# Adaptive-norm attention block with experts on one core: the rotated q and k pass through SBUF instead of PSUM

## The chip, the cores and the metric

The kernel runs on 1 core of one Trainium2 chip. The metric is the device time of one execution in microseconds (us): the median of 3 runs before the change is 937.3 us (936.47 to 941.54).

## What is computed

`reference` is one transformer block over two batches of 1024 tokens with 128 features: a modulated layer norm, attention, a gate and residual, and then a second modulated norm and a mixture of eight experts of which the last chosen one counts. The change concerns the attention alone. In the reference, cut to that:

```python
c_q = h @ w_down_q.T                     # 128 features -> 64
c_kv = h @ w_down_kv.T
q = (c_q @ w_up_q.T).reshape(b, s, 16, 64).transpose(0, 2, 1, 3)
k = (c_kv @ w_up_k.T).reshape(b, s, 16, 64).transpose(0, 2, 1, 3)
v = (c_kv @ w_up_v.T).reshape(b, s, 16, 64).transpose(0, 2, 1, 3)
q = _apply_rope_subspace(q, 64)          # e*cos - o*sin, e*sin + o*cos
k = _apply_rope_subspace(k, 64)
attn = softmax(einsum('bhqd,bhkd->bhqk', q, k) * scale)
out = einsum('bhqk,bhkd->bhqd', attn, v)
```

## The kernel before, in words

The attention goes over 16 pairs of heads: two batches times eight pairs (`NPAIR`), the two heads of a pair side by side on 64 partitions each. Three pairs are in work at once. While pair p has its scores, exponentials and values computed, pair p + 1 has its row maxima computed (they are subtracted from the scores before the exponential), and pair p + 2 has its q and k projected and rotated. The index q in the code below is such a pair.

A pair takes 16 steps (`NSTEP`), each of 128 keys against 512 queries for both heads; steps 0 to 7 belong to the first half of the queries, steps 8 to 15 to the second. Two steps make a group g, 0 to 7; in this text "half" means four groups, 0 to 3 or 4 to 7. The order of every engine is written out by hand in loops over p and g (tensor L484, scalar L673, gpsimd L812, vector L1135, sync L1292). Each engine takes its instructions in that order and waits on semaphores.

In a group TensorE does, in this order: a maxima product for pair p + 1 (`maxima`, L394, both heads into the two banks of `ps_m`); two steps of scores (`score`, L412 to L418, four products each and head: high and low parts of k and q, and the row of maxima); a second maxima product into the same banks; two steps of values times probabilities (`pv`, L428, into `ps_o`); in groups 3 and 7 the denominators (L436); then one up projection for pair p + 2 (`up`, L382, into `ps_x`); and in groups 3 and 7 the output products (L443).

q and k of a pair are made in eight units (`UNITS`) of 256 positions, one per group. For pairs 0 and 1, which are made ahead of the loop, there are four wide units of 512 positions in other banks. For one unit:

- `up` (L364) multiplies the latents with the weights and with the weights whose halves are swapped, into the two halves of the one bank `ps_x` (`unit_banks`, L313): "straight" and "swapped". It first waits until `lower` of the unit before is done, since that reads the bank.
- `turn` (L917) on VectorE: straight times cos in place (L923), swapped times sin into the SBUF buffer `tmp` (L926), and their sum written over straight in PSUM (L928, signal `rotated`).
- `upper` (L619) on ScalarE copies the sum to `q_hi` or `k_hi` as fp32r, its upper bits (L625).
- `lower` (L930) on VectorE subtracts these upper bits from the sum, into `q_lo` or `k_lo` (L934).

VectorE's order in a group is: in groups 0 and 4 the outputs added to x (`out_add`, L1005); the reduction of the first maxima product (`reduce_max`, L941); `turn` of the unit projected in the group before; the reduction of the second; in groups 3 and 7 a small negated maximum (L946); `lower` of the same unit; then in groups 0 and 4 a small reciprocal (`recip`, L993) that waits for a DMA, and in groups 2 and 6 the division of 512 columns of output sums (`divide`, L998: `ou` times `rr`, both in SBUF). `out_add`, `recip` and `divide` run for pair p - 1, so from p = 1 on. The unit turned in group g > 0 is unit g - 1 of pair p + 2, and in group 0 it is unit 7 of pair p + 1. That makes 112 units of 256 in the loop.

A maxima product waits until the reduction of the one before is done, as both use `ps_m`.

GpSimd keeps the sums of probabilities: seven additions per half of 1024 columns, `acc` plus `probs`, all in SBUF (`add`, L794), each once its exponentials are there. Once per pair it splits the weights of a later pair (L761, L763). ScalarE makes the exponentials (L633).

Of the kernel before, what the change touches and what calls it, by code (L numbers as in the profile page):

```python
# [7 lines left out]
ALU = mybir.AluOpType  # L8
ACT = mybir.ActivationFunctionType
AX = mybir.AxisListType  # L10
F32 = mybir.dt.float32
# [3 lines left out]
P = 128  # L15
# [7 lines left out]
QUART = 256  # L23
# [17 lines left out]
def ge(eng, sem, value):  # L41

    if value > 0:
        eng.wait_ge(sem, value)


def build(nc, t, out):
    ctx = ExitStack()
    with ctx:
        def sb(name, shape, dt=F32):  # L50
            return ctx.enter_context(nc.sbuf_tensor(name, shape, dt))
# [4 lines left out]
        def sem(name):  # L56
            return ctx.enter_context(nc.semaphore(name))
# [25 lines left out]
        wh = sb("wh", [P, 2, 2, 2, P], F32R)  # L83
        wl = sb("wl", [P, 2, 2, 2, P], F32R)
        tmp = sb("tmp", [P, HALF])
        q_hi = sb("q_hi", [P, 3, S], F32R)
        q_lo = sb("q_lo", [P, 3, S], F32R)
        k_hi = sb("k_hi", [P, 3, S], F32R)
        k_lo = sb("k_lo", [P, 3, S], F32R)
        hi_of, lo_of = (q_hi, k_hi), (q_lo, k_lo)  # L90
# [96 lines left out]
            "weights_split": "a step of the split of a pair's up projections (gpsimd)",  # L187
            "up_product": "a part of q or k and its swapped twin are in PSUM (tensor)",
            "turned": "a product with cos or sin (vector)",
            "rotated": "their sum: a part of the rotated q or k, in PSUM (vector)",  # L190
            "upper": "its upper bits (scalar)",
            "lower": "its lower bits; its banks are free (vector)",
            "max_product": "both heads' scores of 128 queries for the maxima (tensor)",
            "max_reduced": "their rows' maxima (vector)",
            "max_row": "both heads' maxima of half the queries, negated (vector)",
# [33 lines left out]
        s = {n: sem("s_" + n) for n in signals}  # L229
# [20 lines left out]
        def n_step(p, st):  # L250
            return NSTEP * p + st + 1
# [18 lines left out]
        def n_unit(q, u):  # L270

            return 4 * q + u + 1 if q < 2 else 8 * (q - 1) + u + 1

        def all_units(q):
            return n_unit(q, 3 if q < 2 else 7)

        def unit_columns(q, u):

            if q < 2:
                w, half = WIDE_UNITS[u]  # L280
                return w, slice(half * HALF, (half + 1) * HALF)
            w, quarter = UNITS[u]
            return w, slice(quarter * QUART, (quarter + 1) * QUART)
# [29 lines left out]
        def unit_banks(q, u):  # L313
            return U_BANKS[q][u] if q < 2 else (ps_x[:, 0:QUART], ps_x[:, QUART:HALF])

        def max_banks(q, n):
            return ps_s[:, 2 * (n % 2):2 * (n % 2) + 2, :] if q == 0 else ps_m[:]

        @block.tensor
        def _(pe):  # L320
# [43 lines left out]
            def up(q, u):  # L364

                w, c = unit_columns(q, u)
                if u == 0:
                    pe.wait_ge(s["weights_split"], 2 * (q + 1))
                if q == 0 and u == 2:
                    pe.wait_ge(s["values"], 1)  # L370
                    pe.wait_ge(s["g_copied"], 2)
                if q == 1 and u < 2:
                    pe.wait_ge(s["lower"], n_unit(0, u + 2))
                if q == 1 and u >= 2:
                    pe.wait_ge(s["lower"], n_unit(1, u - 2))
                if q >= 2:
                    pe.wait_ge(s["lower"], n_unit(q, u) - 1)
                b = q // HP
                src = (cq, ck)[w][:, b * S + c.start:b * S + c.stop]
                for twin, bank in enumerate(unit_banks(q, u)):  # L380
                    for n, m in enumerate((wh, wl)):
                        ins = nc.tensor.matmul(bank, m[:, q % 2, w, twin, :], src, start=(n == 0), stop=(n == 1))  # L382
                ins.then_inc(s["up_product"], 1)

            def maxima(q, n):

                qt, kh = max_tile(n)
                pe.wait_ge(s["upper"], units_of_max(q, n))
                if q == 0 and n < 2:
                    pe.wait_ge(s["lower"], n + 1)  # L390
                ge(pe, s["max_reduced"], n - 1 if q == 0 else NMAX * q + n)
                bank = max_banks(q, n)
                for h in range(2):
                    ins = nc.tensor.matmul(bank[:, h, :], q_hi[rows(h), q % 3, qt * P:(qt + 1) * P],  # L394
                                           k_hi[rows(h), q % 3, kh * HALF:(kh + 1) * HALF], start=True, stop=True)
                ins.then_inc(s["max_product"], 1)
# [54 lines left out]
            for u in range(4):  # L451
                up(0, u)
            for n in range(NMAX):
                maxima(0, n)
            for u in range(4):
                up(1, u)
# [27 lines left out]
            for p in range(NPAIR):  # L484
                for g in range(NGRP):
# [27 lines left out]
                    if p + 2 <= LAST:  # L513
                        up(p + 2, g)
# [66 lines left out]
        def _(act):  # L581
# [37 lines left out]
            def upper(q, u):  # L619

                w, c = unit_columns(q, u)
                act.wait_ge(s["rotated"], n_unit(q, u))
                if q >= 3:
                    act.wait_ge(s["scores"], n_step(q - 3, NSTEP - 1))
                nc.scalar.copy(hi_of[w][:, q % 3, c], unit_banks(q, u)[0]).then_inc(s["upper"], 1)  # L625

            def expo(p, st):
                act.wait_ge(s["scores"], n_step(p, st))
# [24 lines left out]
            for u in range(4):  # L653
                upper(0, u)
            root(3)
            for u in range(4):
                upper(1, u)
# [15 lines left out]
            for p in range(NPAIR):  # L673
                for g in range(NGRP):
                    if g == 0 and p > 0:
                        den_out(p - 1, 0, ps_s[:, 2, :])
                    if g == 4 and p > 0:
                        den_out(p - 1, 1, ps_s[:, 2, :])
                    if g == 6 and p == LAST:
                        den_out(p, 0, ps_x[:])  # L680
                    expo(p, 2 * g)
                    expo(p, 2 * g + 1)
                    if g == 0 and 2 <= p + 1 <= LAST:
                        upper(p + 1, NGRP - 1)
                    if g > 0 and p + 2 <= LAST:
                        upper(p + 2, g - 1)
                    if g == 0 and p > 0:
                        o_out(p - 1, 1)
                    if g == 4:
                        o_out(p, 0)  # L690
                    if p == LAST:
                        if g == 0:
                            h2T_out(0)
                        if g == 1:
                            exp_logits(0)
# [148 lines left out]
        def _(dve):  # L844
            seq = [0]
            V = nc.vector
# [70 lines left out]
            def turn(q, u):  # L917

                w, c = unit_columns(q, u)
                straight, swapped = unit_banks(q, u)  # L920
                n = n_unit(q, u)
                dve.wait_ge(s["up_product"], n)
                V.tensor_tensor(straight, straight, cos_sb[:, c], ALU.mult).then_inc(s["turned"], 1)  # L923
                part = tmp[:, 0:c.stop - c.start]
                ge(dve, s["rotated"], n - 1)
                V.tensor_tensor(part, swapped, sin_sb[:, c], ALU.mult).then_inc(s["turned"], 1)  # L926
                dve.wait_ge(s["turned"], 2 * n)
                V.tensor_tensor(straight, straight, part, ALU.add).then_inc(s["rotated"], 1)  # L928

            def lower(q, u):  # L930

                w, c = unit_columns(q, u)
                dve.wait_ge(s["upper"], n_unit(q, u))
                V.tensor_tensor(lo_of[w][:, q % 3, c], unit_banks(q, u)[0], hi_of[w][:, q % 3, c].bitcast(F32),  # L934
                                ALU.subtract).then_inc(s["lower"], 1)

            def reduce_max(q, n):
                qt, kh = max_tile(n)
                dve.wait_ge(s["max_product"], NMAX * q + n + 1)
                ge(dve, s["max_row"], 2 * q + n // TB - 1)  # L940
                V.reduce_max(mx[:, :, kh, qt], max_banks(q, n), AX.X).then_inc(s["max_reduced"], 1)  # L941
# [14 lines left out]

            dve.wait_ge(rot_in, 32)
            turn(0, 0)
            for u in range(1, 4):
                turn(0, u)  # L960
                lower(0, u - 1)
            lower(0, 3)

            for b in range(B):
# [15 lines left out]
            for n in range(8, NMAX):  # L980
                reduce_max(0, n)
            neg_max(0, 1)
            turn(1, 0)
            for u in range(1, 4):
                turn(1, u)
                lower(1, u - 1)
# [148 lines left out]
            for p in range(NPAIR):  # L1135
                for g in range(NGRP):
# [6 lines left out]
                    q, u = (p + 2, g - 1) if g else (p + 1, NGRP - 1)  # L1143
# [269 lines left out]
```

## Time and profile before

| | before |
|---|---|
| median of 3 runs | 937.3 us |
| lowest, highest | 936.47, 941.54 us |
| the profiled execution | 937.06 us, its span 935.1 us |
| busy of that span: TensorE | 823.5 us (88%) |
| VectorE | 665.5 us (71%) |
| GpSimd | 631.1 us (67%) |
| ScalarE | 377.9 us (40%) |
| mean granted TensorE clock | 0.936 |

The profile records one execution. The span goes from its first to its last instruction. Busy time is the union of an engine's instructions; the ends of matmuls are modelled, and the spans of GpSimd's instructions are rough. PE is TensorE, DVE VectorE, ACT ScalarE, POOL GpSimd, SP the sync engine. L934 is line 934 of the kernel. In a row of the timeline, the bracket at the end tells how long the engine stood idle before it and which instruction ended that. The granted clock is a share of TensorE's full speed.

### The profile page before, as it was taken

Reading aid. Unit: us, or ns where it says so; the run is one execution under the profiler, and the core shown is the slowest. Engines: PE = TensorE matmul, PEld = TensorE weight load, DVE = VectorE, ACT = ScalarE, POOL = GpSimd, SP = SyncE. Lnnn points to the kernel's source line nnn. Section 1 sums busy time; section 2 is a strip of 40 time slices with the busy share of each in tenths; the row PEclk is TensorE's granted clock in tenths of the full one; section 3 lists DMA queues with packets and bytes.
Section 4 is the critical chain, followed back from the end, with each engine's and each line's share of the span. In section 5 each row is a group of like instructions: output and inputs, shape, how many; then the busy total and the mean of one; then the engine's idle time right before and its main releaser. Section 6 shows DMA issues by size and latency. Waiting matters only on the chain.

```text
span 935.1 us, 14669 instructions
## 1 busy us (share of the span) xinstructions
PE 823.5 (88%) x5118; PEld 491.9 (53%) x5118; DVE 665.5 (71%) x1198; ACT 377.9 (40%) x622; POOL 631.1 (67%) x324
## 2 busy tenths in 40 slices
PE   4456799999999999999999999999999979859681
PEld 2323455555555555555555555555555445448581
DVE  7896877777777777777777777777777776645122
ACT  3203344444444444444444444444444434316350
POOL 2200897877878787878787878787877777432433
PEclk8756899999999999999999999999999999779796
DMA  7200000101010101101010101111000000058693
GB/s 189 77 0 1 12 12 13 25 13 24 13 24 13 25 13 27 29 16 25 12 24 12 25 14 24 12 24 13 13 13 13 13 13 12 12 185 263 211 335 86
DMA packets 84329, 43.90 MB, mean 47 GB/s; under 512 B 57632, under 2 KB 73376, under 8 KB 84192
## 3 DMA queue, kind: packets, MB, share of 16 engines
q1 hardware_dynamic: 83232, 40.86, 17.1%
q0 software_dynamic: 1024, 2.10, 0.7%
q8 instruction: 42, 0.69, 0.3%
q14 instruction: 31, 0.25, 0.1%
HBM read 36.51 MB, written 6.16 MB: 46 GB/s over the span
## 4 chain that ended last, share of the span: by engine, by line
PE 58%; DVE 24%; issue 5%; DMA 5%; SPq 3%; POOL 2%; ACT 1%; POOLq 0%; DVEq 0%
PE ps_o L428 17%; DVE mx L941 11%; PE ps_x L382 8%; PE ps_m L394 6%; PE ps_s L412 4%; PE ps_s L414 4%; PE ps_s L416 4%; PE ps_s L418 4%; SPq L1254 3%; PE ps_s L443 2%; PE ps_s L436 2%; DMA moe<-xs_dram 2%; DVE tmp L926 2%; POOL xs_dram L808 1%; PE ps_s L538 1%
## 5 line engine op out<-in xcount | busy, mean ns | idle before, releaser
L794 POOL TENSOR_TENSOR acc<-acc,probs 128x1024 f32<-128x1024 f32 (+1 forms) x192 | 458.9, 2390 | 89.5 <-ACT probs L633 69.7
L633 ACT ACTIVATE probs<-ps_s 128x1024 f32<-128x1024 f32 x256 | 248.9, 1023 | 320.0 <-PE ps_s L418 320.0
L941 DVE TENSOR_REDUCE mx<-ps_m 128x2 f32<-128x1024 f32 x240 | 292.5, 1219 | 60.8 <-PE ps_m L394 57.8
L428 PE MATMUL ps_o<-probs,c_all 128*64 128x512 f32 x1024 | 250.0, 609 | 0.0
L428 PEld LDWEIGHTS ps_o<-probs,c_all 128*64 128x64 f32 x1024 | 62.5, 137 | 114.8 <-issue 75.8
L394 PE MATMUL ps_m<-k_hi,q_hi 64*128 64x512 f32 x480 | 108.9, 448 | 9.5 <-issue 6.6
L794 POOL TENSOR_TENSOR acc<-probs 128x1024 f32<-128x1024 f32 (+1 forms) x32 | 75.2, 2350 | 57.8 <-ACT probs L633 57.8
L412 PE MATMUL ps_s<-q_hi,k_hi 64*128 64x512 f32 x512 | 103.4, 399 | 12.0 <-DVE x_sb L1005 10.9
L414 PE MATMUL ps_s<-q_hi,k_lo 64*128 64x512 f32 x512 | 102.2, 394 | 0.0
L418 PE MATMUL ps_s<-neg_row,one_row 64*128 64x512 f32 x512 | 102.0, 393 | 0.0
L416 PE MATMUL ps_s<-q_lo,k_hi 64*128 64x512 f32 x512 | 102.0, 393 | 0.0
L394 PEld LDWEIGHTS ps_m<-k_hi,q_hi 64*128 64x128 f32 x480 | 46.3, 184 | 39.8 <-issue 17.7
L1005 DVE TENSOR_TENSOR x_sb<-x_sb,ps_s 128x512 f32<-128x512 f32 x30 | 20.5, 685 | 61.1 <-PE ps_s L443 61.1
L412 PEld LDWEIGHTS ps_s<-q_hi,k_hi 64*128 64x128 f32 x512 | 49.2, 188 | 24.4 <-issue 17.2
L416 PEld LDWEIGHTS ps_s<-q_lo,k_hi 64*128 64x128 f32 x512 | 49.2, 187 | 10.9
L418 PEld LDWEIGHTS ps_s<-neg_row,one_row 64*128 64x128 f32 x512 | 49.0, 186 | 10.9
L414 PEld LDWEIGHTS ps_s<-q_hi,k_lo 64*128 64x128 f32 x512 | 49.1, 187 | 10.7
L928 DVE TENSOR_TENSOR ps_x<-ps_x,tmp 128x256 f32<-128x256 f32 x112 | 48.4, 432 | 3.8
L926 DVE TENSOR_TENSOR tmp<-ps_x,rot 128x256 f32<-128x256 f32 (+1 forms) x115 | 48.4, 421 | 0.0
L382 PEld LDWEIGHTS ps_x<-ck,wh 128*128 128x128 f32 x112 | 21.0, 188 | 51.6 <-DVE k_lo L934 26.1
L923 DVE TENSOR_TENSOR ps_x<-ps_x,rot 128x256 f32<-128x256 f32 x112 | 47.3, 422 | 0.0
L382 PEld LDWEIGHTS ps_x<-cq,wh 128*128 128x128 f32 x115 | 21.8, 190 | 47.4 <-DVE k_lo L934 23.9
(264 smaller groups left out, 1024.9 us busy)
## 6 DMA issues: line engine op xcount, KB each, us to landing
probs<-in_experts SPq DMA_DIRECT2D x15, 578.0 KB, 5.6
rr<-rd_dram SPq DMA_DIRECT2D x62, 128.0 KB, 3.0
wu<-in_wqk SPq DMA_DIRECT2D x16, 256.0 KB, 3.2
neg_row<-nm SPq DMA_DIRECT2D x256, 0.5 KB, 2.0
w_first<-in_experts SPq DMA_DIRECT2D x5, 578.0 KB, 5.0
rot<-in_experts SPq DMA_DIRECT2D x5, 578.0 KB, 5.2
hT<-in_experts SPq DMA_DIRECT2D x5, 578.0 KB, 5.7
xs_dram<-zero SPq DMA_DIRECT2D x2, 960.0 KB, 6.1
```

What stands on the lines that cost most here:

```text
L382: ins = nc.tensor.matmul(bank, m[:, q % 2, w, twin, :], src, start=(n == 0), stop=(n == 1))
L394: ins = nc.tensor.matmul(bank[:, h, :], q_hi[rows(h), q % 3, qt * P:(qt + 1) * P], k_hi[rows(h), q % 3, kh * HALF:(kh + 1) * HALF], start= ...
L412: nc.tensor.matmul(bank[h], k_hi[rows(h), p % 3, kc], q_hi[rows(h), p % 3, qc], start=True, stop=False)
L414: nc.tensor.matmul(bank[h], k_lo[rows(h), p % 3, kc], q_hi[rows(h), p % 3, qc], start=False, stop=False)
L416: nc.tensor.matmul(bank[h], k_hi[rows(h), p % 3, kc], q_lo[rows(h), p % 3, qc], start=False, stop=False)
L418: ins = nc.tensor.matmul(bank[h], one_row[rows(h), :], neg_row[rows(h), p % 2, qc], start=False, stop=True)
L428: ins = nc.tensor.matmul(ps_o[64 * h:64 * h + 64, :], c_all[:, (p // HP) * TB + kt, :], probs[:, st % 4, h, :], start=(kt == 0), stop=(kt ...
L633: nc.scalar.activation(probs[:, st % 4, :, :], ps_s[:, 2 * (st % 2):2 * (st % 2) + 2, :], ACT.Exp, scale=SCALE).then_inc(s["probs"], 1)
L794: V.tensor_tensor(acc[:, half, heads, :], first, probs[:, st % 4, heads, :], ALU.add).then_inc(s["added"], 1)
L926: V.tensor_tensor(part, swapped, sin_sb[:, c], ALU.mult).then_inc(s["turned"], 1)
L928: V.tensor_tensor(straight, straight, part, ALU.add).then_inc(s["rotated"], 1)
L941: V.reduce_max(mx[:, :, kh, qt], max_banks(q, n), AX.X).then_inc(s["max_reduced"], 1)
```

## The change

The sum of the rotation goes to a new SBUF buffer `rsum` of two slots of 256 columns, for all pairs from 2 on. `upper` and `lower` read it there. The up projection then waits for the sum (`rotated`) of the unit before instead of its `lower`, and VectorE waits, before a sum, for the `lower` of two units back, which read the same slot. Pairs 0 and 1 keep their sums in PSUM; the first projection of pair 2 waits for the last `lower` of pair 1. No instruction is added or removed but for waits.

```diff
+        rsum = sb("rsum", [P, 2, QUART])
...
+        def rotated_in(q, u):
+            return unit_banks(q, u)[0] if q < 2 else rsum[:, u % 2, :]
+
...
                 if q == 1 and u >= 2:
                     pe.wait_ge(s["lower"], n_unit(1, u - 2))
+                if q == 2 and u == 0:
+                    pe.wait_ge(s["lower"], all_units(1))
                 if q >= 2:
-                    pe.wait_ge(s["lower"], n_unit(q, u) - 1)
+                    pe.wait_ge(s["rotated"], n_unit(q, u) - 1)
...
-                nc.scalar.copy(hi_of[w][:, q % 3, c], unit_banks(q, u)[0]).then_inc(s["upper"], 1)
+                nc.scalar.copy(hi_of[w][:, q % 3, c], rotated_in(q, u)).then_inc(s["upper"], 1)
...
                 dve.wait_ge(s["turned"], 2 * n)
-                V.tensor_tensor(straight, straight, part, ALU.add).then_inc(s["rotated"], 1)
+                if q >= 2:
+                    ge(dve, s["lower"], n_unit(q, u) - 2)
+                V.tensor_tensor(rotated_in(q, u), straight, part, ALU.add).then_inc(s["rotated"], 1)
...
-                V.tensor_tensor(lo_of[w][:, q % 3, c], unit_banks(q, u)[0], hi_of[w][:, q % 3, c].bitcast(F32),
+                V.tensor_tensor(lo_of[w][:, q % 3, c], rotated_in(q, u), hi_of[w][:, q % 3, c].bitcast(F32),
                                 ALU.subtract).then_inc(s["lower"], 1)
```

## Rows read from the trace of the kernel before

**Rows 1.** Stretch, length; busy us of PE, PEld, DVE, ACT, POOL; granted clock.

```profile
105.00:725.00 620.00, 614.78 (x3896) 348.55 (x3896) 476.51 (x777) 278.97 (x390) 504.44 (x223) 1.00 0.10 18
```

**Rows 2.** Timeline of PE, a plain group: start us, us, engine, line, operation, tiles.

```profile
421.90 1.94 PE L428 MATMUL ps_o<-probs,c_all 128*64 128x512 f32 x8
423.78 0.39 PE L382 MATMUL ps_x<-cq,wh 128*128 128x256 f32 x1
...
426.62 0.40 PE L394 MATMUL ps_m<-k_hi,q_hi 64*128 64x512 f32 x2
```

**Rows 3.** Timeline of DVE, groups 0 to 3 of a pair.

```profile
409.72 1.22 DVE L941 TENSOR_REDUCE mx<-ps_m 128x2 f32<-128x1024 f32 x1
...
411.63 0.43 DVE L928 TENSOR_TENSOR ps_x<-ps_x,tmp 128x256 f32<-128x256 f32 x1
...
413.11 0.41 DVE L934 TENSOR_TENSOR q_lo<-ps_x,q_hi 128x256 fp32r<-128x256 f32 x1
414.25 0.20 DVE L993 RECIPROCAL rc<-denc 128x8 f32<-128x8 f32 x1 [0.73 <-DMA denc<-den]
414.84 1.23 DVE L941 TENSOR_REDUCE mx<-ps_m 128x2 f32<-128x1024 f32 x1 [0.39 <-PE ps_m L394]
...
419.92 1.23 DVE L941 TENSOR_REDUCE mx<-ps_m 128x2 f32<-128x1024 f32 x1 [1.27 <-PE ps_m L394]
...
423.31 0.41 DVE L934 TENSOR_TENSOR k_lo<-ps_x,k_hi 128x256 fp32r<-128x256 f32 x1
423.64 1.24 DVE L998 TENSOR_TENSOR ou<-ou,rr 128x512 f32<-128x512 f32 x1
424.99 1.23 DVE L941 TENSOR_REDUCE mx<-ps_m 128x2 f32<-128x1024 f32 x1
```

**Rows 4.** Timeline of PE, group 0 of the same pair and the start of group 1.

```profile
411.22 0.40 PE L394 MATMUL ps_m<-k_hi,q_hi 64*128 64x512 f32 x2
...
412.02 1.46 PE L428 MATMUL ps_o<-probs,c_all 128*64 128x512 f32 x6
413.67 0.36 PE L382 MATMUL ps_x<-ck,wh 128*128 128x256 f32 x1 [0.19 <-DVE q_lo L934]
...
416.48 0.39 PE L394 MATMUL ps_m<-k_hi,q_hi 64*128 64x512 f32 x2
```

**Rows 5.** L934: duration ns min/median/max, first and last start; who waited (us, times).

```profile
L934 DVE TENSOR_TENSOR q_lo<-ps_x,q_hi x56: 410/414/417, 119.2 to 725.0; 128x256 fp32r<-128x256 f32 x56
...
  PEld ps_x L382: 83.7, 97
```

**Rows 6.** The same view of L998, and the group of L926 by shape.

```profile
L998 DVE TENSOR_TENSOR ou<-ou,rr x31: 676/1227/2694, 156.5 to 826.5; 128x512 f32<-128x512 f32 x31
...
L926 DVE TENSOR_TENSOR tmp<-ps_x,rot 128x256 f32<-128x256 f32 x112 | 46.3, 414 | 0.0
```

**Rows 7.** Timeline of ACT, the cast to upper bits in group 0.

```profile
412.34 0.37 ACT L625 CAST q_hi<-ps_x 128x256 fp32r<-128x256 f32 x1
```

**Rows 8.** Timeline of POOL, adds beside the `lower` of groups 0 and 2.

```profile
412.52 2.36 POOL L794 TENSOR_TENSOR acc<-probs 128x1024 f32<-128x1024 f32 x1 [2.64 <-ACT probs L633]
...
421.97 2.37 POOL L794 TENSOR_TENSOR acc<-acc,probs 128x1024 f32<-128x1024 f32 x1 [0.20 <-ACT probs L633]
...
424.48 2.66 POOL L794 TENSOR_TENSOR acc<-acc,probs 128x1024 f32<-128x1024 f32 x1
```

**Rows 9.** Timeline of DVE and POOL, a small product of the router beside an add.

```profile
784.57 2.23 DVE L1077 TENSOR_TENSOR rt_sb<-rt_sb,rs 128x64 f32<-128x64 f32 x1
...
784.34 2.38 POOL L794 TENSOR_TENSOR acc<-acc,probs 128x1024 f32<-128x1024 f32 x1
```

**Rows 10.** Timeline of DVE and POOL ahead of the loop, both reading SBUF.

```profile
92.84 3.25 DVE L1012 TENSOR_TENSOR x_sb<-x_sb,h 128x1024 f32<-128x1024 f32 x1
...
92.11 2.90 POOL L779 TENSOR_TENSOR hT<-acc,mod 128x1024 f32<-128x1024 f32 x1 [58.52 <-PE ps_s L360]
...
94.97 3.32 POOL L779 TENSOR_TENSOR hT<-acc,mod 128x1024 f32<-128x1024 f32 x1
```

More of the change, by code:

```diff
@@ L189, in build @@
             "turned": "a product with cos or sin (vector)",
-            "rotated": "their sum: a part of the rotated q or k, in PSUM (vector)",
+            "rotated": "their sum: a part of the rotated q or k (vector)",
             "upper": "its upper bits (scalar)",
-            "lower": "its lower bits; its banks are free (vector)",
+            "lower": "its lower bits (vector)",
             "max_product": "both heads' scores of 128 queries for the maxima (tensor)",
```

## The prediction, made before the changed kernel had run

> **What bounds the kernel now.** I began with the engines' busy time over the attention loop. From 105 to 725 us TensorE is busy 614.8 of 620.0 us at a granted clock of 1.00, the upper of its two levels (2.4 GHz), VectorE 476.5 and GpSimd 504.4 [rows 1]. So in these 620 us nearly everything that makes the time longer is a hole in TensorE's stream, and VectorE has 23% to spare on average. The average hides where it has none, so I went on to the timeline of half a pair, four groups of two steps, 22.3 us long.
>
> In a plain group TensorE ends its eight value matmuls at 421.90 + 1.94 = 423.84, and the first matmul of the up projection starts at 423.78, 0.06 before that modelled end [rows 2]. The projection waits for `lower`, which ended at 423.31 + 0.41 = 423.72 [rows 3]. Wait and stream end together: nothing is lost. In the first group of a half (g = 0 and 4), VectorE first adds the outputs to x, so all it does is later: `lower` ends at 413.52 [rows 3], the value matmuls ended at 412.02 + 1.46 = 413.48, the projection starts at 413.67 [rows 4]. Against the plain group's 0.06 before the end, 0.25 us are lost. The waits "for L934" look like more, 83.7 us over 97 times [rows 5], but that is idle time of the weight loads, most of which lies under matmuls still running.
>
> VectorE's slack: before the first maxima of group 2 it stands idle 1.27 us, and of group 1 0.39 us; after the divide (L998), which stands right behind `lower` in groups 2 and 6, only 0.11 us pass between 424.88 and the next maxima at 424.99 [rows 3].
>
> **What is removed.** TensorE's wait moves from `lower` to `rotated`, ready about 1.5 us earlier (the sum of 411.63 ends at 412.06, `lower` at 413.52) [rows 3]. The projection then starts 0.06 before the end of the value matmuls everywhere. That gives 0.25 us (0.2 to 0.3) in 27 first groups (g = 0 and 4), about 6.8 us, and 0.01 (0 to 0.03) in 84 others, 1 us. Ceiling: 8 us.
>
> **The sum into SBUF.** One operand stays in PSUM; the same form with an SBUF result is L926, 414 ns against 0.43 us [rows 3, 6]: nothing, at best 0.02 us. The added wait of VectorE on its own `lower` two units back is long satisfied; one more wait instruction, 0 to 0.03 us, in VectorE's slack. The first projection of q = 2 now also waits for the last `lower` of q = 1, which lies ahead of the attention loop. ScalarE reads its 256 columns from SBUF instead of PSUM: the cast ends at 412.71, 0.40 us before `lower` starts [rows 3, 7], so a difference of up to 0.4 either way is covered; if that cover went, `lower` would start later by the rest.
>
> **`lower` from SBUF.** This is the cost. Today it has one PSUM and one SBUF operand and takes 410 to 417 ns [rows 5], although a GpSimd add runs beside it (from 412.52 to 414.88 and from 421.97 to 424.34; nearly all of the other 110 lie like one of these two) [rows 3, 8]. Afterwards both operands are in SBUF. VectorE has such instructions, and they behave otherwise. The divide, 512 columns, started at 423.64 and ended at 424.88, 0.54 after the add that ended at 424.34; the next add, issued at 424.48, took 2.66 instead of 2.37 and so ended 2.26 after the divide [rows 3, 8]. Its median is 1227 ns, its extremes 676 and 2694 [rows 6]. A product of only 64 columns takes 2.23 us, from 784.57 to 786.80, and an add runs from 784.34 to 786.72 [rows 9]. I read this as: an operation with two SBUF inputs stands still until GpSimd's running add has ended, and then streams (512 columns in 0.54, so 256 in 0.27). Bounds for `lower`: 0.41 if there is no such exclusion, 2.37 + 0.27 = 2.64 if the add has just begun. By the positions of today's adds, the rest of the add is 1.03 us in most groups and 1.77 in g = 0 and 4, so `lower` takes about 1.3 and 2.0 us.
>
> The Trainium skill, page "SBUF — State Buffer", section "Who interferes with whom", says that a Vector instruction with two SBUF inputs contends with a GpSimd instruction that reads SBUF, and that the one issued first gets the shared ports for the whole instruction. By that rule the time is the forecast's or rival 1's, and not rival 2's 930 us; the trace agrees with it in the 2.23 us for 64 columns. Which of two waiting instructions is served first it does not say, and on this hangs most of the sum.
>
> Who waits for the longer `lower`? In groups 1, 3, 5, 7 (and 2, 6 without a divide) nobody: 0.9 more against 1.27 of slack, or, in groups 3 and 7, before the outputs that come later. Two places remain.
>
> *Groups 0 and 4.* `lower` is asked for at 413.11, the add ends at 414.88, `lower` at 415.15. The reciprocal starts 0.08 before that (as the divide does behind `lower` today), the next maxima 0.12 later: 415.19 instead of 414.84 [rows 3, 8]. They end at 416.41, and the matmuls that reuse the bank follow 0.28 later (maxima 409.72 + 1.22 = 410.94, matmul 411.22) [rows 3, 4]: 416.69 instead of 416.48 [rows 4]. So 0.21 us, in which the gain of the earlier projection is already eaten. 26 times: +5.5 us.
>
> *Groups 2 and 6 with a divide.* `lower` ends at 424.34 + 0.27 = 424.61. The next add has been asking since 424.48 (0.14 behind the last), the divide only since 424.53. If the add goes first it ends at 424.61 + 2.26 = 426.87, the divide at 427.41, 2.53 later than today. The next maxima start at 427.33 and end at 428.55, and the matmuls that need the bank start at 428.83 instead of 426.62 [rows 2]: a hole of 2.2 us in TensorE's stream. Of the 31 divides [rows 6], 26 stand behind a `lower` (pairs 1 to 13, two each): +57 us. Bounds: 0 and 2.5 us each.
>
> Does the add go first? Both engines stand in line ahead of the loop [rows 10]: the add of 92.11 ends at 95.01, GpSimd's next was issued at 94.97, before that end, and yet the waiting L1012 went first (it ended at 96.09, and the second add took 3.32). The one that has waited longer wins over the holder's next instruction. I take that.
>
> **Sum.** 26 x 2.2 + 26 x 0.21 - 84 x 0.01 = 57.2 + 5.5 - 0.8, about +62. In such a half the later adds still end before they are needed: GpSimd gains 2.2 us of room per half and loses 0.5. A small part of the hole may be won back where positions shift, so I take +60. The profiled execution took 937.06 us (span 935.1), and the median of the runs is 937.3, the same within 0.03%: 997 us. Own range, with holes of 1.9 to 2.5 us and 0 to 9 for the rest: 986 to 1011.
>
> **Rivals.**
> 1. *VectorE keeps its turn behind `lower`* (the divide streams directly, 424.61 to 425.14; maxima from 425.06 end at 426.28, matmul by 426.56, in time for 426.62). Then only groups 0 and 4 cost, less 0.8: 937 + 5.5 - 0.8, about 942 (938 to 948). For it: the divide is issued while `lower` is still streaming, and the add leads by just 0.05 us. Against it: the order seen ahead of the loop [rows 10].
> 2. *No exclusion for this form*, the other side: `lower` stays at 0.4 us, the projection gains its 6.8 + 1 us, about 930 (928 to 933). It decides as long as the holes stay under 7.8 / 28 = 0.28 us per half. For it: `lower` writes fp32r and reads two small buffers, which no row shows in this pairing. Against it: the divide and the product of 64 columns, on either side of its 256 in size [rows 3, 9].
> 3. *Worse positions.* The order of adds and `lower` shifts so that the add has always just begun: 2.64 instead of 0.41 is 2.23 more, against 1.27 of slack and 0.12 at the bank (424.99 + 1.23 + 0.28 = 426.50 against 426.62), so 0.84 us in the 58 of the 84 groups that have no divide, 49 on top of the forecast: about 1046. Against it: TensorE's scores set the start of adds and of VectorE's chain alike, so their distance stays.
>
> **Chances.** Forecast 0.70; rival 1 0.13; rival 2 0.08; rival 3 0.09. What a measurement of this kernel can tell from no change is about 0.5%, 4.7 us. Rival 1 straddles that bound (0.09 within, 0.04 above); rival 2 gives nearly all of faster (0.07, and 0.01 within). So faster 0.07, same 0.10, slower 0.83. The range that leaves out no more than 2 in 10 takes forecast and rival 1: 938 to 1012.
>
> **What would show it.** Right: `lower` at about 1.3 us median, up to 2; the divide at about 2.9 us; TensorE idle before the second maxima matmuls (L394) of groups 3 and 7 for 2.2 us, released by L941, some 26 times; the projection no longer released by `lower`; clock still 1.00. Wrong: a divide of 0.6 us directly behind `lower` (rival 1), `lower` at 0.41 (rival 2), or holes in every group (rival 3).

## The result, and the profile after

| | before | after |
|---|---|---|
| median | 939.32 us (4 runs) | 1014.38 us (4 runs) |
| lowest, highest | 936.47, 941.54 us | 1010.98, 1015.27 us |
| the profiled execution | 937.06 us, span 935.1 | 1010.98 us, span 1009.0 |
| mean granted clock | 0.936 | 0.926 |

The changed kernel takes 1.080 times as long (95% interval 1.077 to 1.084), 75 us more. Forecast were 997 us and a range of 938 to 1012: the direction and the place are right, the amount is 15 to 17 us short, and the median lies 2.4 us above the range.

The totals of the page, then its groups that the change touches (busy us, mean ns, then idle time just before them):

```profile
PE 846.2 (84%) x5118; PEld 497.9 (49%) x5118; DVE 814.6 (81%) x1198; ACT 387.2 (38%) x622; POOL 633.7 (63%) x324
...
L942 DVE TENSOR_TENSOR q_lo<-rsum,q_hi 128x256 fp32r<-128x256 f32 x56 | 88.5, 1580 | 0.0
L1006 DVE TENSOR_TENSOR ou<-ou,rr 128x512 f32<-128x512 f32 x31 | 81.4, 2625 | 5.4 <-DMA rr<-rd_dram 5.4
L942 DVE TENSOR_TENSOR k_lo<-rsum,k_hi 128x256 fp32r<-128x256 f32 x56 | 68.2, 1217 | 0.0
...
L936 DVE TENSOR_TENSOR rsum<-ps_x,tmp 128x256 f32<-128x256 f32 x112 | 47.5, 424 | 3.9
```

Against the table of before, VectorE is busy 149 us longer (814.6 against 665.5), with the same work. I read this as waiting and not as streaming: an instruction that stands still until GpSimd's add has ended counts as busy, and experiment 1 bears it out. The sum itself costs nothing more in SBUF (424 ns). `lower` (L942) had 414 ns [rows 5] and the divide (L1006) 1227 ns median [rows 6]; the source view of the same two lines now gives minimum, median and maximum as

```profile
L942 DVE TENSOR_TENSOR k_lo<-rsum,k_hi x56: 414/1228/2552, 109.7 to 778.8; 128x256 fp32r<-128x256 f32 x56
L942 DVE TENSOR_TENSOR q_lo<-rsum,q_hi x56: 1103/1484/2208, 120.2 to 797.8; 128x256 fp32r<-128x256 f32 x56
...
L1006 DVE TENSOR_TENSOR ou<-ou,rr x31: 677/2878/2884, 159.2 to 900.7; 128x512 f32<-128x512 f32 x31
```

Predicted were 1.3 and 2.0 us for `lower`, about 2.9 for the divide. The timeline of one half of a pair shows the chain: GpSimd's adds, then VectorE, then TensorE (start, length, and in brackets the idle time before it).

```profile
406.11 2.37 POOL L800 TENSOR_TENSOR acc<-acc,probs 128x1024 f32<-128x1024 f32 x1 [0.53 <-ACT probs L639]
...
408.62 2.40 POOL L800 TENSOR_TENSOR acc<-acc,probs 128x1024 f32<-128x1024 f32 x1
...
411.16 2.62 POOL L800 TENSOR_TENSOR acc<-acc,probs 128x1024 f32<-128x1024 f32 x1
...
407.47 1.29 DVE L942 TENSOR_TENSOR k_lo<-rsum,k_hi 128x256 fp32r<-128x256 f32 x1
408.68 2.88 DVE L1006 TENSOR_TENSOR ou<-ou,rr 128x512 f32<-128x512 f32 x1
411.49 1.21 DVE L949 TENSOR_REDUCE mx<-ps_m 128x2 f32<-128x1024 f32 x1
...
397.44 0.39 PE L388 MATMUL ps_x<-ck,wh 128*128 128x256 f32 x1
...
402.87 0.38 PE L388 MATMUL ps_x<-ck,wh 128*128 128x256 f32 x1
...
407.89 0.39 PE L388 MATMUL ps_x<-cq,wh 128*128 128x256 f32 x1
...
408.56 0.50 PE L400 MATMUL ps_m<-k_hi,q_hi 64*128 64x512 f32 x2
...
412.85 0.49 PE L400 MATMUL ps_m<-k_hi,q_hi 64*128 64x512 f32 x2 [1.95 <-DVE mx L949]
...
416.00 0.38 PE L388 MATMUL ps_x<-ck,wh 128*128 128x256 f32 x1
```

Read it from the first add. It ends at 408.48; `lower`, asked for at 407.47, streams then and ends at 408.76, 0.28 later. The second add was issued at 408.62, the divide at 408.68, 0.06 after it and both while `lower` was still at work. The add goes first: it ends at 411.02, 2.26 after `lower`. The divide ends at 411.56, 0.54 after that. The maxima (L949) start at 411.49 instead of right after `lower`, and TensorE stands idle 1.95 us before the second maxima matmul. In the group before, which has no hole, the second follows 2.15 us behind the first; here that would be 410.71, so it is 2.14 late. The view of waits counts such stops (us in total, times, the longest; 26 of the 37 are the holes behind a divide that stands behind a `lower`):

```profile
PE ps_m L400 <- DVE mx L949: 57.3, 37, 2.0
```

I took the starts of the first projection matmul as a clock of the loop. In this half they are 5.43, 5.02 and 8.11 us apart. Medians over the 26 halves with a divide behind a `lower`, one value for each of the four groups: before 6.13 (6.22 in every second half), 5.06, 5.07 and 5.90, after 5.93, 5.42, 5.03 and 8.10. The differences are -0.20 to -0.29, +0.36, -0.04 and +2.20. A whole half has a median of 22.23 us before, and of 24.49 after in the 17 halves whose clock is 1.00 throughout: 2.26 more, 59 us in 26 halves. The first to last projection of pairs 2 and on took 616.3 us before and 689.6 after, 73.3 more. So 14 us are left that the ordinary half does not explain. Views of the windows, for two neighbouring halves and one earlier (length; busy us of PE, PEld, DVE, ACT, POOL; granted clock), show where most of them are:

```profile
437.40:461.90 24.50, 22.42 (x142) 12.67 (x142) 22.47 (x29) 10.34 (x14) 16.89 (x8) 1.00 0.09 12
461.90:488.00 26.10, 24.05 (x142) 12.92 (x142) 22.43 (x29) 10.33 (x14) 19.52 (x10) 0.93 0.12 22
236.90:263.10 26.20, 24.12 (x140) 12.98 (x141) 22.47 (x29) 10.32 (x14) 16.88 (x8) 0.93 0.08 12
```

The second half has the same 142 matmuls as the first and is 1.6 us longer, its clock 0.93. The timeline of TensorE at the start of the third one:

```profile
236.93 0.50 PE L400 MATMUL ps_m<-k_hi,q_hi 64*128 64x512 f32 x2 [1.94 <-DVE mx L949]
237.36 3.06 PE L434 MATMUL ps_o<-probs,c_all 128*64 128x512 f32 x8
240.20 1.65 PE L442 MATMUL ps_s<-acc,ones 128*64 128x512 f32 x4
```

The eight value matmuls take 3.06 us instead of 1.94, the denominators 1.65 instead of 1.03 as in undisturbed halves: close behind a hole TensorE runs for a while at the lower of its two levels (1.2 GHz). There are seven such spells in these halves (from 238.0, 313.1, 463.3, 538.4, 613.5, 688.6 and 739.8 us), each 1.1 to 1.5 us behind the end of one of the holes, and none in the loop of the kernel before. At about 1.7 us each they are 12 of the 14 us. Another 1.3 us lie in the first four projections of the loop (17.55 us for 16.30), ahead of any hole, where a spell of the lower clock starts at 104.9 us. That is not shown to come from the change: `b_tiny_adds` and `b_filler1` below, which do not have it, take 17.86 us there. The last 1 us I did not place.

### The profile page after: what moved, and what is told of

It reads as the page before. It is cut to its first block, busy times and chain, and to the rows that moved or that the text cites. A ratio compares the mean times of both kernels' runs of the same rounds, so it can differ in the third digit from the quotient of the medians.

```text
span 1009.0 us, 14781 instructions
## 1 busy us (share of the span) xinstructions
PE 846.2 (84%) x5118; PEld 497.9 (49%) x5118; DVE 814.6 (81%) x1198; ACT 387.2 (38%) x622; POOL 633.7 (63%) x324
## 3 DMA queue, kind: packets, MB, share of 16 engines
q0 software_dynamic: 1024, 2.10, 0.6%
## 4 chain that ended last, share of the span: by engine, by line
PE 48%; DVE 27%; issue 13%; DMA 5%; SPq 3%; POOL 2%; ACT 1%; POOLq 0%; DVEq 0%
PE ps_o L434 16%; DVE mx L949 10%; PE ps_m L400 6%; PE ps_x L388 5%; PE ps_s L418 3%; PE ps_s L424 3%; PE ps_s L422 3%; PE ps_s L420 3%; SPq L1262 3%; PE ps_s L442 2%; DVE q_lo L942 2%; PE ps_s L449 2%; DVE k_lo L942 2%; DMA moe<-xs_dram 2%; DVE tmp L932 2%
## 5 line engine op out<-in xcount | busy, mean ns | idle before, releaser
L949 DVE TENSOR_REDUCE mx<-ps_m 128x2 f32<-128x1024 f32 x240 | 291.0, 1213 | 33.2 <-PE ps_m L400 33.2
L434 PE MATMUL ps_o<-probs,c_all 128*64 128x512 f32 x1024 | 257.2, 624 | 0.0
L400 PE MATMUL ps_m<-k_hi,q_hi 64*128 64x512 f32 x480 | 114.3, 467 | 66.1 <-DVE mx L949 57.3
L942 DVE TENSOR_TENSOR q_lo<-rsum,q_hi 128x256 fp32r<-128x256 f32 x56 | 88.5, 1580 | 0.0
L1006 DVE TENSOR_TENSOR ou<-ou,rr 128x512 f32<-128x512 f32 x31 | 81.4, 2625 | 5.4 <-DMA rr<-rd_dram 5.4
L942 DVE TENSOR_TENSOR k_lo<-rsum,k_hi 128x256 fp32r<-128x256 f32 x56 | 68.2, 1217 | 0.0
L936 DVE TENSOR_TENSOR rsum<-ps_x,tmp 128x256 f32<-128x256 f32 x112 | 47.5, 424 | 3.9
```

What stands on the lines that cost most here:

```text
L434: ins = nc.tensor.matmul(ps_o[64 * h:64 * h + 64, :], c_all[:, (p // HP) * TB + kt, :], probs[:, st % 4, h, :], start=(kt == 0), stop=(kt ...
L942: V.tensor_tensor(lo_of[w][:, q % 3, c], rotated_in(q, u), hi_of[w][:, q % 3, c].bitcast(F32), ALU.subtract).then_inc(s["lower"], 1)
L1006: V.tensor_tensor(ou[:, half, :], ou[:, half, :], rr[:, half, :], ALU.mult).then_inc(s["divided"], 1)
```

## The experiments

Eleven kernels ran, in three groups; each group had its own runs of the kernel before beside it (medians 936.6, 938.4 and 932.7 us, the last a single run). "After" and "before" say on which kernel an edit was made. Single runs are good for some 4 us: the kernel before itself ranged from 933.3 to 941.5 in the first group.

**1, 2. Without GpSimd's share.** The adds of all pairs but the first are cut to 8 columns of a head, so most of the softmax sums is left out, in both kernels.

```diff
-                V.tensor_tensor(acc[:, half, heads, :], first, probs[:, st % 4, heads, :], ALU.add).then_inc(s["added"], 1)
+                cols = slice(0, 8 if p else HALF)
+                V.tensor_tensor(acc[:, half, heads, cols], first[:, :, cols], probs[:, st % 4, heads, cols], ALU.add).then_inc(s["added"], 1)
```

> The changed kernel with GpSimd's additions of pairs 1 to 15 cut from 512 to 8 columns per head (their sums, and with them the denominators, are left out in part). Theory T (lower waits for GpSimd's running add because both read SBUF): with adds of some 0.2 us lower falls to 0.4 to 0.6 us, the divide to about 0.7, no hole before the second maxima, no spell at the half clock in the loop; about 930 us, up to 8 below the same cut in the kernel before. Rival R1 (two SBUF inputs are slow by themselves, or the copy of ScalarE from SBUF is): lower stays above 1 us and the time above 960.

> The kernel before with the same additions cut to 8 columns. Both theories: TensorE's stream is full already, so 930 to 937 us, and lower at 0.41 us as before. It is the base for the cut version of the changed kernel: T expects that one 0 to 8 us below this, R1 at least 25 above.

Measured: after 913.73 us, before 923.87. The loss is gone: beside short adds the change gains 10 us. The source view of `lower` and the divide:

```profile
L943 DVE TENSOR_TENSOR k_lo<-rsum,k_hi x56: 414/415/1399, 111.5 to 702.6; 128x256 fp32r<-128x256 f32 x56
...
L1007 DVE TENSOR_TENSOR ou<-ou,rr x31: 681/685/693, 158.5 to 800.6; 128x512 f32<-128x512 f32 x31
```

`lower` itself has nothing slow about it. Whatever it gained comes from GpSimd's adds. Both absolute times are below what was expected: behind the last projection the cut kernel before took 200.1 us and the whole one 215.8; I did not take that apart. The 10 us are a difference of two single runs. In their traces a half is 0.30 us shorter on average (21.96 for 22.26), 8 us in 26 halves, which is what the earlier projection was to give at most.

**3, 4. The same work in another order.** GpSimd's add of the sixth step of a half (`kt == 5`, the fifth of its seven adds) waits for the divide (`a_order`, the first two lines); in `a_order2` the first add (`kt == 1`) also waits for the `lower` of the half's first group (the last two).

```diff
                 pool.wait_ge(s["probs"], n_step(p, st))
+                if kt == 5 and 1 <= p <= LAST - 2:
+                    pool.wait_ge(s["divided"], n_part(p - 1, half))
+                if kt == 1 and (half or p >= 1) and p <= LAST - 1 - half:
+                    pool.wait_ge(s["lower"], n_unit(p + 2, 3) if half else n_unit(p + 1, 7))
```

> The changed kernel; GpSimd's sixth step add of each half (kt = 5) of pairs 1 to 13 also waits until the divide of the pair before is done. Nothing else is changed. T (the hole is the divide standing behind that add): the divide behind lower falls from 2.88 to 0.7 us, the 2 us hole in groups 3 and 7 is gone, the clock stays at 1.00 in the loop, 940 to 948 us. R2 (the longer lower itself, in every group, costs the time): it stays above 990 us, since lower waits as before.

> As a_order, and the first add of each half also waits for the lower of the first group (g = 0 and 4). T: the late start of the maxima in groups 1 and 5 goes too and the earlier projection shows: 929 to 938 us, below or level with the kernel before. If the wait of the add passes on to later adds of the half, up to 942. R2: above 980.

Measured: `a_order` 935.95 us (10 runs), 0.998 of before (0.996 to 1.000); `a_order2` 931.45 us (927.78 to 933.11, 8 runs), 0.995 of before (0.994 to 0.997). One wait takes back all of the 75 us (940 to 948 was expected). With the holes the spells of the lower clock are gone too: it is 1.00 from 108 to 767 us. The source view of `a_order`, and its timeline at the place:

```profile
L944 DVE TENSOR_TENSOR q_lo<-rsum,q_hi x56: 1094/1798/2197, 120.4 to 723.7; 128x256 fp32r<-128x256 f32 x56
...
L1008 DVE TENSOR_TENSOR ou<-ou,rr x31: 676/679/2720, 158.0 to 825.4; 128x512 f32<-128x512 f32 x31
```

```profile
421.31 2.37 POOL L802 TENSOR_TENSOR acc<-acc,probs 128x1024 f32<-128x1024 f32 x1 [0.53 <-ACT probs L639]
...
424.69 2.39 POOL L802 TENSOR_TENSOR acc<-acc,probs 128x1024 f32<-128x1024 f32 x1 [1.01 <-DVE ou L1008]
...
422.66 1.30 DVE L944 TENSOR_TENSOR k_lo<-rsum,k_hi 128x256 fp32r<-128x256 f32 x1
423.88 0.68 DVE L1008 TENSOR_TENSOR ou<-ou,rr 128x512 f32<-128x512 f32 x1
424.48 1.21 DVE L951 TENSOR_REDUCE mx<-ps_m 128x2 f32<-128x1024 f32 x1
```

`lower` is as long as in the changed kernel (1.30 us here), and costs next to nothing by itself. Only the divide behind it has become short, 0.68 us for 2.88, and the hole is gone: the long `lower` was the occasion, the add that went between it and the divide was the cost. In the loop from 105 to 725 us TensorE is busy 617.4 us with `a_order` and, at a clock of 1.00, nearly all of the time with `a_order2`:

```profile
105.00:725.00 620.00, 619.25 (x3938) 354.89 (x3934) 548.38 (x783) 286.09 (x395) 504.97 (x225) 1.00 0.10 18
```

Before it was 614.78 [rows 1].

**5. The control for that gain.** Both waits in the kernel before.

> The kernel before with both waits of a_order2 in GpSimd's adds and nothing of the change: control. T: lower has a PSUM operand and no need of the port, so the waits only hold GpSimd back; the divide behind lower falls from 1.24 to 0.7 us, which nobody waits for: 936 to 941 us, the same as before. If instead the gain of a_order2 comes from the waits and not from the earlier projection: 930 to 933.

Measured: 936.44 us (10 runs), 0.999 of before (0.997 to 1.001). So the waits alone bring nothing, and the 0.5% of `a_order2` need the change. A detail of the expectation did not hold: the divide stayed at a mean of 1.27 us, because the add that runs when it is asked for still holds it.

**6. A `lower` of 16 columns.** From pair 3 on only 16 of the 256 columns of the lower bits are computed (the others are left out).

```diff
+                if q >= 3:
+                    c0 = slice(c.start, c.start + 16)
+                    V.tensor_tensor(lo_of[w][:, q % 3, c0], rotated_in(q, u)[:, 0:16],
+                                    hi_of[w][:, q % 3, c0].bitcast(F32), ALU.subtract).then_inc(s["lower"], 1)
+                    return
```

> The changed kernel with lower cut from 256 to 16 columns for pairs 3 to 15 (the other columns of q_lo and k_lo stay as they were: left out). T (at the port, who has asked first goes first): lower now streams for 0.02 us after GpSimd's add ends, so the divide asks before GpSimd's next add does, 0.14 after the last; it streams directly, 0.6 to 0.8 us instead of 2.88, for 24 of 26 divides, and the hole is gone though lower still waits about 1 us for the add: 936 to 950 us. R3 (GpSimd's next add goes first whenever both want the port): the divide stays at 2.6 to 2.9 us and the time within 10 us of the changed kernel's.

Measured: 935.46 us. In its timeline:

```profile
424.14 1.06 DVE L944 TENSOR_TENSOR k_lo<-rsum,k_hi 128x16 fp32r<-128x16 f32 x1
425.12 0.68 DVE L1011 TENSOR_TENSOR ou<-ou,rr 128x512 f32<-128x512 f32 x1
425.81 1.23 DVE L954 TENSOR_REDUCE mx<-ps_m 128x2 f32<-128x1024 f32 x1
```

The 16 columns still take 1.06 us, so the time of `lower` is waiting, not size. But the divide behind it now goes first (0.68 us). The reading that fits: with so little to stream `lower` ends sooner behind the add, at 425.20, and GpSimd's next add is issued only at 425.31, so nothing stands in the divide's way. With 256 columns that add was issued 0.14 us before `lower` ended. A tenth or two of a microsecond decide over 75 us.

What this does not show is the rule by which two waiting instructions are served. The first to ask may go first, as the prediction had it, or the turn may simply pass to the other engine whenever it is asking. In the changed kernel, in experiment 10 and in [rows 10], where both engines have asked, the instruction served next is both the first to ask and not of the engine that was served last. A `lower` of about 160 columns would tell the two apart. By an estimate from these rows (some 1 ns a column, 0.08 before the end for the divide, 0.14 behind the add for GpSimd) the divide would then ask first, and the add still before `lower` ends. It was not run.

**7, 8, 9. Holes without the change.** To price a hole alone, the kernel before got reductions of a constant behind each of the 26 divides, which delay the next maxima as the late divide does: two of 1024 columns in `b_filler` (without the last line of the diff), one in `b_filler1`, and two and a short one in `b_filler_long`.

```diff
                             divide(p - 1, g // 4)
+                            if p <= LAST - 2:
+                                for _ in range(2):
+                                    V.reduce_max(scr[:, _, :], ones_w[:], AX.X)
+                                V.reduce_max(scr[:, 2, :], ones_w[:, :, 0:150], AX.X)
```

> The kernel before, with two reductions of 128x1024 ones (one SBUF input, no port) behind each of the 26 divides that have a lower in front: VectorE comes 2.26 us late to the first maxima of groups 3 and 7, as in the changed kernel, and nothing else changes. T (the loss is VectorE's lateness there): holes of 2.0 us before the second maxima, 52 us, and spells of the half clock behind some of them that add 5 to 15 us more: 990 to 1008 us. R4 (the clock spells come from something else in the change): 52 us alone, clock 1.00 in the loop, 988 to 992.

> The same with one reduction: 1.13 us late less the slack of 0.23, holes of 0.9 us, 26 times: 23 us, so 958 to 964 us. Whether the clock falls in the loop with holes of this size is open: if spells come with any hole, up to 975.

Measured: `b_filler` 987.36 us, `b_filler1` 958.39, with a granted clock of 1.00 in the loop of both. I had expected spells of the lower level in `b_filler`, and there are none. Its waits are 1.60 us, shorter than the 1.95 of the changed kernel (timeline, and the half that follows in the view of windows):

```profile
426.20 0.50 PE L396 MATMUL ps_m<-k_hi,q_hi 64*128 64x512 f32 x2 [1.60 <-DVE mx L944]
```

```profile
426.20:450.30 24.10, 22.30 (x140) 12.71 (x140) 19.35 (x31) 10.10 (x14) 16.86 (x8) 1.00 0.09 12
```

That left open whether the spells come with the length of the hole or with something of the changed kernel. A third filler of 300 columns brings the holes to the same length:

> The kernel before with a third, short filler (150 columns for each of two rows of ones, about 0.35 us) behind the two: idle stretches of TensorE before the second maxima of groups 3 and 7 of about 1.95 us instead of 1.6, as long as in the changed kernel. T5 (the spells at the half clock follow from the length of these holes): some spells in the loop as in the changed kernel, 26 x 2.2 + 5 to 15 = 999 to 1010 us. R5 (they come from something else in the change, such as its fuller stream between the holes): clock 1.00 in the loop and 994 to 998 us.

Measured: 1008.15 us. That is 75.5 above the run of before beside it, where `b_filler` was 49.0 above its own: 26 us more, from single runs (21 if the two fillers are compared directly). The timeline of one hole, and two neighbouring halves in the view of windows:

```profile
409.85 0.51 PE L396 MATMUL ps_m<-k_hi,q_hi 64*128 64x512 f32 x2 [1.97 <-DVE mx L944]
```

```profile
434.20:458.70 24.50, 22.30 (x140) 12.60 (x141) 19.77 (x32) 10.12 (x14) 16.92 (x8) 1.00 0.08 12
458.70:484.80 26.10, 24.04 (x140) 12.85 (x140) 19.63 (x32) 10.13 (x14) 19.38 (x10) 0.93 0.11 22
```

The two halves are copies of those of the changed kernel, 24.5 and 26.1 us at clocks of 1.00 and 0.93, in a kernel that has no `rsum`. Nine spells stand in its loop. The longer hole explains 26 x 0.4 = 10 of the 21 to 26 us, the spells 9 x 1.7 = 15. So in these runs the spells come with the longer holes, and need nothing else of the change.

**10. The divide in front of `lower`** in groups 2 and 6 of the changed kernel.

```diff
+                    if p > 0 and g in (2, 6):
+                        divide(p - 1, g // 4)
                     if 2 <= q <= LAST:
                         lower(q, u)
                     if p > 0:
                         if g in (0, 4):
                             recip(p - 1, g // 4)
-                        if g in (2, 6):
-                            divide(p - 1, g // 4)
```

> The changed kernel with the divide put in front of lower in groups 2 and 6. T: the divide takes about 1.24 us again, as before, but lower then stands behind the add that asked while the divide streamed: lower 2.6 us there, the hole stays, 1000 to 1018 us. R6 (the divide is what suffers, being long): the hole goes, 940 to 950 us.

Measured: 1014.34 us, as the changed kernel. The timeline of VectorE:

```profile
408.80 1.57 DVE L1006 TENSOR_TENSOR ou<-ou,rr 128x512 f32<-128x512 f32 x1
410.29 2.61 DVE L942 TENSOR_TENSOR k_lo<-rsum,k_hi 128x256 fp32r<-128x256 f32 x1
412.82 1.21 DVE L949 TENSOR_REDUCE mx<-ps_m 128x2 f32<-128x1024 f32 x1
```

The divide now gets the first turn (1.57 us, where 1.24 was expected), and `lower`, a quarter of a microsecond of streaming, pays a whole add (2.61). It is not a matter of either operation: two such instructions in a row pay one rest of an add and one whole add, 4.2 us in both orders (1.29 + 2.88, 1.57 + 2.61). This kernel has nine spells behind holes of 1.92 to 1.94 us.

**11. The projection waits for `lower` again** in the changed kernel; the sum stays in SBUF.

```diff
-                    pe.wait_ge(s["rotated"], n_unit(q, u) - 1)
+                    pe.wait_ge(s["lower"], n_unit(q, u) - 1)
```

> The changed kernel with only the projection's wait undone: it waits for lower of the unit before, as in the kernel before. T: now the longer lower is on TensorE's path in every group, 0.9 us in groups 1, 2, 5, 6, 1.5 in 0 and 4, some tenths in 3 and 7, besides the holes: 1050 to 1110 us. R7 (the earlier projection is worth nothing even now): within 5 us of the changed kernel.

Measured: 1095.33 us, 81 more than the changed kernel. Its waits (us in total, times, the longest):

```profile
PE ps_x L388 <- DVE q_lo L942: 66.9, 54, 1.8
PE ps_x L388 <- DVE k_lo L942: 50.9, 48, 1.7
```

Once the sum is in SBUF, the moved wait is worth 81 us instead of 8: the two parts of the change can't be priced one by one from the kernel before. Seven spells stand in its loop as well, each behind a hole of 1.73 to 1.83 us at a projection; a half has one such hole there, besides some four of 0.8 to 1.2 us.

## Why the prediction was right in kind and short in size

- *Removed wait, 7.8 us.* Right: the projection no longer waits for `lower` (its source view names `lower` 114 times as what ended TensorE's idle time before it, and 4 times after the change), and the first group of a half is 0.20 to 0.29 us shorter (0.25 forecast). With short adds the change gains 10 us, 8 of them in the halves.
- *Sum into SBUF, nothing.* Right, 424 ns. The same holds for the cast: `lower` starts no later for it.
- *`lower` about 1.3 and 2.0 us.* Right where it mattered: medians of 1.29 in groups 2 and 6 and of 2.04 in groups 0 and 4. In groups 1 and 5 it was 0.75 and in groups 3 and 7 1.49, where 1.3 stood and nobody waits. The exclusion with GpSimd's reads is shown by experiments 1, 2 and 6. The Trainium skill, page "SBUF — State Buffer", section "Who interferes with whom", gives the exclusion for a Vector instruction with two SBUF inputs; the trace agrees, with 415 ns beside short adds and 1228 beside long ones. Rival 2, which needed the opposite, falls.
- *Groups 0 and 4, 0.21 us each.* 0.07 to 0.16 was measured (-0.20 to -0.29, and +0.36), so 2 to 4 us in all and not 5.5.
- *Groups 2 and 6, the add goes ahead of the divide, 2.2 us each.* Right in mechanism and size: the add goes first; 2.88 us for the divide (about 2.9 forecast) and 2.20 us per half. The rule behind it, that the one that has waited longer wins, was read from a single pair of rows [rows 10] and stays open: no run here tells it from taking turns (experiment 6), and both give this forecast. Rival 1 falls; `a_narrow_lower` is what it would have looked like. Rival 3 falls too: no hole came in the groups without a divide.
- *Own sum.* +59 us of ordinary halves were measured where +62 stood, and +60 was taken.
- **The step that failed** is the last line of the sum, which had no term for the granted clock, and the sentence "clock still 1.00" that went with it. I took the clock of the loop before [rows 1] for a property of the kernel, and did not ask what the holes that I forecast would do to it. Seven spells at the lower level, 1.7 us each, are 12 us. Experiment 9 puts such spells behind the same holes in a kernel without the change, and experiment 3 takes holes and spells out together. 59 + 12 is 71 of the 73 us that the loop got longer by (1.3 of the rest lie ahead of the holes and are not shown to be the change's), and 937.1 + 73.9 is the profiled execution. The median is another 3.4 us above it, with a spread of 4.3 between runs. Two more spells would make up for that: `a_swap`, at 1014.3 us, has nine, and the three executions without a trace had mean clocks of 0.922 to 0.924, the profiled one 0.926. It is not shown, since only one execution has a trace.
- *Range.* It ended 1012, since the upper bound of a hole (2.5 us) was counted and the clock was not. Another 2 us of the miss are the kernel before, whose median a fourth run moved from 937.3 to 939.3.

## What to carry to other kernels

Before an operand is moved from PSUM to SBUF, look whether GpSimd runs beside the instruction that reads it: a VectorE instruction that then has two SBUF inputs waits for the running GpSimd instruction, and two of them in a row can pay another whole one, here 75 us for a change of place that costs its writer nothing. Then look at who asks next on each side; a wait that lets GpSimd come behind the second VectorE instruction gave all of it back (1014.4 to 936.0 us), and a second wait made the change a gain (931.5 us, 0.5% below the kernel before). And when a forecast puts repeated holes of about two microseconds into a dense matmul stream, give the sum a term for the clock: here 12 to 15 us, by seven to nine spells.

## What the runs showed of the hardware that was not expected

- Of 26 holes in the changed kernel, all but one of 1.92 to 1.95 us and with some 22 us of dense matmuls between them, seven were followed by a spell at 1.2 GHz, of 26 of 1.97 us nine (`b_filler_long`), of 26 of 1.60 us none (`b_filler`). The length of one hole is not all there is to it: in `a_oldwait`, with more holes in a half, seven of 26 holes of 1.73 to 1.83 us were followed by one. In the changed kernel the first six spells start 75.1, 150.2, 75.1, 75.1 and 75.1 us apart, the last 51.2. What picks the hole I can't say from these traces.
- VectorE issues the next instruction 0.08 us before the recorded end of its last, GpSimd 0.14 after, and still GpSimd's add was 0.06 ahead of the divide: `lower` streams for 0.27 us behind the add, in which GpSimd's next is already asking. That fits with 16 columns being enough to turn the order and 256 not.
- A waiting instruction shows as busy with a longer duration and no idle time before it. The "0.0" behind L942 in the page's groups says nothing about its waits; the spread between minimum and median (414 and 1228 ns) does.
